# Weights laid out by the host, low parts of the FFN pieces on GpSimd, and a smaller preparing section

## The chip, the cores and the metric

The kernel runs on one core of a Trainium2 chip. The metric is the device time of one execution in microseconds (us). A core has TensorE (PE, matmuls; PEld is its weight load), VectorE (DVE), ScalarE (ACT), GpSimd (POOL) and SyncE (SP), which here only issues DMAs. Each engine takes its instructions in the order in which the program lists them and waits on semaphores.

## The reference

`x` has 4 x 2048 tokens of 512 channels. One layer: token-shifted linear attention with decay per head (32 heads of 16), then an FFN of 2048 hidden channels.

```python
xx = pad(ln(x))[:, :T] - ln(x);  xk, xv, xr, xg = ln(x) + xx * time_maa_{k,v,r,g}
r, k, v = xr @ Wr.T, xk @ Wk.T, xv @ Wv.T;  g = silu(xg @ Wg.T)
# chunks of Q tokens: yc = (rc @ kc * w_mat) @ vc + rc @ state * wb;  state = ws * state + kc * wk @ vc
x = x + (groupnorm(y) * gamma + beta) * g @ Wo.T
D = gelu(fp16(ln(x)) @ W0.T + bias0);  x = x + fp16(fp16(D) @ W1.T + bias1)
```

## The kernel before, in words

The kernel works in fp16 pairs: every weight and most activations are split into a high part (fp16 of the scaled value) and a low part (fp16 of what is left), and each product is made in three passes (two for the FFN).

**The preparing section** (`prepare()`) is a block of its own with a barrier behind it that all engines pass together. It loads x of the first 256 tokens and the five attention weights (1 MB each), has ACT square each for its scale (L493), PE average the sums over partitions (L504), DVE turn this into a power of two (`dve_scale`, six small operations). PE transposes each weight from rows to columns (L617; V is centred by the same matmul, L615), ACT writes the high half from PSUM (L516), and DVE the low half (L423); eight of the ten DVE halves stand in the section, the two of O behind it. SP also issues the loads of the eight 512 KB pieces of W0.

**The steps.** Behind the barrier each engine runs a list of steps n = 0 to 34, written out by hand (`pe_step`, `dve_step`, `act_step`, `pool_step`, `sp_step`). A step handles attention for block n of 256 tokens, the tail of attention of block n-1 and the FFN of block n-2. So steps 0 and 1 have no FFN work yet, and from step 3 on (`*_steady`) all steps are alike. In one step DVE does, among others: `mixf` (L279, 16 of them, from `dx` and `xnT`), low parts of `mix` (L339), `dx` (L270), `att32` (L1350, "weigh", from PSUM), low parts of `att` (L1356), the state S (L1382, four of 64 columns per chunk, four chunks), and y from PSUM (L1400, L1411, L1413). POOL makes the low part of `vw` (L2002), of the gated y (L1982) and of S (`Shl`, L1988). The low part of S after chunk c is waited for by DVE's S of chunk c+1 and by PE's `pe_from_state`.

**The FFN weights** come as 16 pieces (8 of W0, then 8 of W1), prepared in steps 0 and 1 at the places of `PREPARED_AT`: ACT writes the scaled high part (L828) and, for the first nine, a diagonal matrix of the scale (L819). PE makes the transposed low part as piece x diagonal minus high x identity (L847, L851), ACT copies it out of PSUM (L862), and SP transposes the high part by DMA (L872) and stores pieces 5 to 15 to `w_dram` (L882), from where they are streamed each step. DVE and ACT use `xh`, `e16` and `vw32` as places for high parts.

Of the kernel before, what the change touches and what calls it, by code (L numbers as in the profile page):

```python
# [12 lines left out]
P = 128  # L13
# [81 lines left out]
def program(nc, ctx, a, consts, x, out, wd, nb):  # L95
# [33 lines left out]
    maa = sb("maa", [P, 4, G])  # L129
# [7 lines left out]
    gam = sb("gam", [P, G])  # L137
    bet = sb("bet", [P, G])
# [3 lines left out]
    b0 = sb("b0", [P, NH])  # L142
# [14 lines left out]

    B = ps("B", [P, C])
# [206 lines left out]
    def parts_of(q):  # L365

        return place_of(q)[:, 0:2 * C], place_of(q)[:, 2 * C:4 * C]

    def stashed(j):

        return 32 if j < KEPT else 64

    def sp_raw(eng, n, j):
        if n == 0:
            source = W0[2 * P * j:2 * P * (j + 1), :]
        else:
            if j >= KEPT:
                eng.wait_ge(s_stash[j], 32)
            source = W1[:, 2 * P * j:2 * P * (j + 1)]
        if n == 0:  # L380
            eng.dma_start(raw_piece(PIECES * n + j).rearrange("p (b c) -> p b c", b=2),
                          source.rearrange("(b p) c -> p b c", p=P)).then_inc(s_raw[j], 16)
        else:
            for i in range(2):
                eng.dma_start(raw_piece(PIECES * n + j)[:, C * i:C * i + C].rearrange("p (b c) -> p b c", b=G),
                              source[:, P * i:P * i + P].rearrange("(b p) c -> p b c", p=P)).then_inc(s_raw[j], 16)

    def act_piece_square(eng, n, j, squares):
        q = PIECES * n + j
        eng.wait_ge(s_raw[j], 48 if n else 16)  # L390
# [52 lines left out]

    def prepare():
# [3 lines left out]
        raw = sb("raw", [P, 5, G, C], F32, own)  # L448
        centring = sb("centring", [P, P], F32, own)
        junk = sb("junk", [P, G * C], F32, own)  # L450
        sums = sb("sums", [P, 5], F32, own)
        means = sb("means", [P, P], F32, own)
# [11 lines left out]
        tp = (F[:, :, :], own.enter_context(nc.psum_tensor("tp1", [P, 2, C], F32))[:, :, :], Y)  # L464
        landed = [own.enter_context(nc.semaphore(f"landed{u}")) for u in range(5)]
        s_tab, s_means, s_sum, s_all, s_tr, s_hi = (
            own.enter_context(nc.semaphore(f"s_{v}")) for v in ("tab", "means", "sum", "all", "tr", "hi"))
        s_scl = [own.enter_context(nc.semaphore(f"s_scl{u}")) for u in ORDER]
# [3 lines left out]
        def full(u):  # L472
            return 16 * (G + 2) if u in (K_, R_) else 16

        def load(eng, u):

            if u in (K_, R_):
# [352 lines left out]
    def pe_prepare(eng, n, place):  # L830

        q = piece(n, place)
        if q is None:
            return
# [1422 lines left out]
```

## Time and profile before

| | us |
|---|---|
| Median of 3 runs (2046.63 to 2051.36) | 2048.89 |
| The profiled execution's own time | 2050.78 |
| Its span | 2049.0 |
| Preparing section, to the first matmul of step 0 | 43.3 |
| Step 0 and step 1 by DVE's list | 63.9 and 64.8 |
| A step of the steady kind | 60.1 |

The span is what the profile covers; the time of the execution is 1.8 us longer. Row times are from the span's start. In a timeline row, "x8" means that eight instructions of one kind ran one behind the other, and the second number is what they took together; the bracket is the engine's idle time ahead of it and what ended that.

### The profile page before, as it was taken

The numbers are of one execution on the slowest core, as the hardware profiler recorded it, in microseconds if no ns is written. First come the engines' busy times: TensorE is split into PE (matmuls) and PEld (weight loads), VectorE is DVE, ScalarE is ACT, GpSimd is POOL, SyncE is SP. The second block draws the span as 40 slices with busy tenths as digits, with TensorE's granted clock in tenths as the row PEclk, the third lists the DMA queues.
The fourth block names the chain that finished last, engine by engine and source line by source line (L and its number), as shares of the span: only waits on it lengthen the run. The fifth ranks groups of instructions, "written<-read, shape, count | busy, mean of one in ns | idle before, by whom it ended". The sixth has DMA issues, their size and how long they took to land.

```text
span 2049.0 us, 64453 instructions
## 1 busy us (share of the span) xinstructions
PE 1999.8 (98%) x27206; PEld 1424.3 (70%) x27206; DVE 1738.7 (85%) x3687; ACT 1293.0 (63%) x2081; POOL 317.5 (15%) x329
## 2 busy tenths in 40 slices
PE   5889999999999999999999999999999999999999
PEld 4767667777666777766777766667776677777676
DVE  7778889888888888888988888888888898888771
ACT  7775566676555677656667656667765666766452
POOL 1011111111111111111111111111111111111110
PEclk8999999999999999999999999999999999999999
DMA  6776666777666677766667766667777666776656
GB/s 217 161 193 194 177 178 182 199 197 196 177 194 171 189 198 195 185 190 189 173 194 202 199 174 186 181 181 202 192 195 184 191 180 185 199 202 177 181 175 191
DMA packets 403216, 385.42 MB, mean 188 GB/s; under 512 B 256880, under 2 KB 304112, under 8 KB 402928
## 3 DMA queue, kind: packets, MB, share of 16 engines
q1 hardware_dynamic: 401296, 381.12, 68.1%
q8 instruction: 215, 3.52, 0.7%
q14 instruction: 73, 0.60, 0.1%
q10 hardware_dynamic: 1632, 0.18, 0.1%
HBM read 232.32 MB, written 22.54 MB: 124 GB/s over the span
## 4 chain that ended last, share of the span: by engine, by line
PE 81%; SPq 4%; DVE 4%; ACT 4%; DMA 3%; issue 2%; POOL 0%; ACTq 0%; DVEq 0%
PE F L1149 19%; PE F L1086 16%; PE B L892 9%; PE B L1053 8%; PE sc L892 7%; PE YT L924 6%; PE YT L892 3%; DMA y<-ygT 3%; PE YT L976 3%; SPq L2044 2%; PE sc L954 2%; PE YT L995 2%; PE YT L1086 1%; PE F L847 1%; PE YT L1025 1%
## 5 line engine op out<-in xcount | busy, mean ns | idle before, releaser
L1149 PE MATMUL F<-ring,hT 128*128 128x512 f16 x1984 | 467.7, 379 | 0.5 <-issue 0.5
L1149 PEld LDWEIGHTS F<-ring,hT 128*128 128x128 f16 x1984 | 189.1, 98 | 198.4 <-issue 0.8
L1086 PE MATMUL F<-xT,kept 128*128 128x256 f16 x2400 | 276.8, 273 | 2.0 <-issue 1.2
L892 PE MATMUL B<-mix,WT 128*128 128x256 f16 x2304 | 267.5, 273 | 0.0
L1785 ACT ACTIVATE hT<-F,b,f_rho 128x256 f16<-128x256 f32 x480 | 243.4, 560 | 37.8 <-PE F L1086 37.7
L1086 PEld LDWEIGHTS F<-xT,kept 128*128 128x128 f16 x2400 | 234.6, 98 | 42.1 <-issue 2.6
L892 PEld LDWEIGHTS B<-mix,WT 128*128 128x128 f16 x2304 | 222.7, 98 | 33.3 <-DVE gT L1389 0.3
L279 DVE SCALAR_TENSOR_TENSOR mixf<-dx,maa,xnT 128x256 f32<-128x256 f32 x512 | 238.7, 527 | 0.1
L1742 ACT ACTIVATE Shl<-S 128x256 f16<-128x256 f32 x128 | 53.1, 415 | 236.2 <-PE YT L995 125.8
L1988 POOL TENSOR_TENSOR Shl<-S,Shl 128x256 f16<-128x256 f32 x128 | 89.2, 697 | 708.5 <-ACT Shl L1742 702.1
L1736 ACT ACTIVATE att<-att 128x512 f16<-128x512 f32 x256 | 147.5, 624 | 67.7 <-DVE att L1350 67.7
L339 DVE TENSOR_TENSOR mix<-mixf,mix 128x1024 f16<-128x1024 f32 x128 | 184.1, 1438 | 3.2 <-ACT mix L335 2.2
L892 PE MATMUL sc<-mix,WT 128*128 128x256 f16 x1536 | 180.4, 275 | 3.0 <-PEq L577 3.0
L1356 DVE TENSOR_TENSOR att<-att 128x512 f16<-128x512 f32 x256 | 166.8, 693 | 17.2 <-ACT att L1736 17.0
L924 PE MATMUL YT<-WT,mix 128*128 128x512 f16 x768 | 178.6, 383 | 1.3 <-DVE mix L339 0.9
L1086 PE MATMUL F<-xT,ring 128*128 128x256 f16 x1440 | 172.5, 273 | 4.1 <-ACT hT L1785 4.1
L1053 PE MATMUL B<-WT,yg 128*128 128x512 f16 x768 | 176.5, 379 | 0.0
L1350 DVE TENSOR_TENSOR att<-sc,wmask 128x512 f32<-128x512 f32 x256 | 164.3, 684 | 13.3 <-PE sc L954 13.1
L892 PEld LDWEIGHTS sc<-mix,WT 128*128 128x128 f16 x1536 | 151.0, 99 | 34.6 <-issue 3.6
L1993 POOL TENSOR_TENSOR x<-e,x 128x512 f32<-128x512 f16 x62 | 70.7, 1161 | 578.0 <-DVE e L1429 578.0
L1086 PEld LDWEIGHTS F<-xT,ring 128*128 128x128 f16 x1440 | 135.3, 98 | 23.3 <-issue 6.4
L335 ACT ACTIVATE mix<-mixf 128x1024 f16<-128x1024 f32 x128 | 134.6, 1051 | 5.1 <-DVE mixf L279 4.2
(208 smaller groups left out, 3108.6 us busy)
## 6 DMA issues: line engine op xcount, KB each, us to landing
ring<-w_dram SPq DMA_DIRECT2D x352, 512.0 KB, 3.7
kx<-kT SPq DMA_DIRECT2D x96, 256.0 KB, 3.8
rx<-rT SPq DMA_DIRECT2D x96, 256.0 KB, 4.5
xa<-in_L_attn_x SPq DMA_DIRECT2D x32, 512.0 KB, 5.0
vbd<-vN SPq DMA_DIRECT2D x256, 64.0 KB, 2.1
x<-in_L_attn_x SPq DMA_DIRECT2D x32, 512.0 KB, 5.0
out<-x SPq DMA_DIRECT2D x31, 512.0 KB, 3.5
kept<-in_L_ffn_W SPq DMA_DIRECT2D x5, 512.0 KB, 12.0
```

The costliest lines, as they stand in the source:

```text
L279: last = eng.scalar_tensor_tensor(out=mixf[:, m % 2, g, :], in0=dx[:, g, :], scalar=maa[:, m, g:g + 1], in1=xnT[:, g, 1:BT + 1], op0=ALU.m ...
L335: eng.activation(mix[:, m % 2, 0, :, :], mixf[:, m % 2, :, :], ACT.Copy).then_inc(s_mh, 1)
L339: eng.tensor_tensor(mix[:, m % 2, 1, :, :], mixf[:, m % 2, :, :], mix[:, m % 2, 0, :, :], ALU.subtract).then_inc(s_ml, 1)
L892: mm = eng.matmul(out[:, gg * BT:(gg + 1) * BT], WT[:, w, a, kk, rows(g)], mix[:, m % 2, b, kk, :], start=(i == 0 and kk == 0), stop=(i == ...
L924: mm = eng.matmul(Y[:, t, :], mix[:, 0, a, kk, rows(t)], WT[:, V_, b, kk, :], start=(i == 0 and kk == 0), stop=(i == 2 and kk == G - 1))
L1053: mm = eng.matmul(B[:, :], yg[:, a, kk, rows(t)], WT[:, O_, b, kk, :], start=(i == 0 and kk == 0), stop=(i == 2 and kk == G - 1))
L1086: mm = eng.matmul(up_place(f, j)[:, i * BT:(i + 1) * BT], w, xT[:, :, kk, :], start=(kk == 0 and a == 0), stop=(kk == G - 1 and a == 1))
L1149: mm = eng.matmul(F[:, t, :], hT[:, k, rows(t)], ring[:, use % RING, i, a * C:(a + 1) * C], start=(k == 0 and a == 0), stop=(k == NH - 1 a ...
L1350: eng.tensor_tensor(att32[:, x, :], sc[:, x, :], wmask[:, 8 * x:8 * x + 8, :].rearrange("p q i -> p (q i)"), ALU.mult).then_inc(s_am, 1)
L1356: eng.tensor_tensor(att[:, c % 2, 1, C * x:C * x + C], att32[:, x, :], att[:, c % 2, 0, C * x:C * x + C], ALU.subtract).then_inc(s_al, 1)
L1736: eng.activation(att[:, c % 2, 0, C * x:C * x + C], att32[:, x, :], ACT.Copy).then_inc(s_ah, 1)
L1785: eng.activation(hT[:, k, :], up_place(f, j)[:, i * BT:(i + 1) * BT], ACT.Gelu, bias=b0[:, k:k + 1], scale=f_rho[:, j:j + 1]).then_inc(s_h, 1)
```

## The change

- The host lays out all weights but Wv with input channels on partitions, already permuted, and W0 and W1 piece by piece; maa, gamma, beta and bias0 come as one table `cols`. Wr and Wk are one DMA each instead of six.
- In the preparing section PE transposes nothing; it only centres V. High and low halves of K and R are made there from SBUF. Those of V, G and O move into step 0 (`act_late_hi`, `dve_late_lo`). `dve_scale` for V, G and O is one set of six operations on three columns. POOL's memsets of S, Shl, kx, rx and vbd move into the section.
- PE's, ACT's and SP's share in the low parts of FFN pieces goes: no L847, L851, L819, L862, and no DMA transposes. POOL makes each with two instructions (`pool_low`): the piece times its scale, 1024 columns in fp32, in place, then minus the high part, into fp16. Pieces 0 to 4 stand behind `vw` of step 0, 5 and 6 behind `Shl` of chunk 0, 7 behind that of chunk 1; step 1 has 8 to 11, 12 and 13, 14, 15 in the same way.

```diff
+HIGH_AT = ({"X": (2,), "V1": (3,), "sc0": (4,), "state0": (5,), "sc1": (6,), "sc2": (7,)},
+           {"X": (8, 9), "V1": (10,), "sc0": (11,), "G0": (12,), "sc1": (13,), "state1": (14,), "sc2": (15,)})
+LOW_AT = ({"vw1": (0, 1, 2, 3, 4), "state0": (5, 6), "state1": (7,)},
+          {"vw1": (8, 9, 10, 11), "state0": (12, 13), "state1": (14,), "state2": (15,)})
...
+    def pool_low(eng, n, place):
+        if n < 2:
+            for q in LOW_AT[n].get(place, ()):
+                k = min(q, PIECES)
+                eng.wait_ge(s_phi, q + 1)
+                eng.tensor_scalar(raw_piece(q), raw_piece(q), f_scl[:, k:k + 1], None, ALU.mult).then_inc(s_psc, 1)
+                eng.wait_ge(s_psc, q + 1)
+                eng.tensor_tensor(low_place(q), raw_piece(q), high(q), ALU.subtract).then_inc(s_plo, 1)
...
@@ the preparing section, ACT
                 for half in range(2):
                     act_hi(eng, R_, half)
-                act_square(eng, G_)
-                act_hi(eng, V_, 0)
-                act_square(eng, O_)
-                act_hi(eng, V_, 1)
                 act_exps(eng, 1)
                 act_fades(eng)
-                for half in range(2):
-                    act_hi(eng, G_, half)
+                act_square(eng, G_)
                 act_mix_hi(eng, 0, 1)
-                for half in range(2):
-                    act_hi(eng, O_, half)
+                act_square(eng, O_)
@@ the preparing section, DVE
-                dve_scale(eng, V_)
                 for half in range(2):
                     dve_lo(eng, R_, half)
-                dve_lo(eng, V_, 0)
-                dve_scale(eng, G_)
-                dve_lo(eng, V_, 1)
-                dve_scale(eng, O_)
-                for half in range(2):
-                    dve_lo(eng, G_, half)
                 dve_tables_rest(eng)
+                dve_scale(eng, V_)
@@ dve_step, step 0 (places in its order)
                 mix_lo(eng, 0, 1)
+                for half in range(2):
+                    dve_late_lo(eng, V_, half)
...
-                dve_weight_lo(eng, O_, 0, Y)
...
-                dve_weight_lo(eng, O_, 1, F[:, :, :])
...
                 dve_factors(eng)
+                for half in range(2):
+                    dve_late_lo(eng, G_, half)
...
             dve_take_y(eng, n, 1)
+        if n == 0:
+            for half in range(2):
+                dve_late_lo(eng, O_, half)
@@ pool_step
                 eng.tensor_tensor(vw[:, t, 1, :], vw32[:, :], vw[:, t, 0, :], ALU.subtract).then_inc(s_vwl, 1)
+            pool_low(eng, n, "vw1")
...
                 pool_state_lo(eng, n, c)
+                pool_low(eng, n, f"state{c}")
```

POOL's queue before, from the barrier to the first `Shl` of step 1 (`vw` is the weighted V, `Shl` the parts of the state, `yg` the gated y):

```order
L2204 MEMSET vbd 128x2048
L2002 ISA
L2002 TENSOR_TENSOR vw<-vw 128x512 x2
L1988 TENSOR_TENSOR Shl<-S,Shl 128x256 x4
L2002 TENSOR_TENSOR vw<-vw 128x512 x2
L1982 TENSOR_TENSOR yg<-ygT,yg 128x4x128 x2
L1988 TENSOR_TENSOR Shl<-S,Shl 128x256 x4
```

The same queue now, in step 0 (the line of dots stands for the pairs of pieces 1 to 4, which read like that of piece 0):

```order
L1924 TENSOR_TENSOR vw<-vw 128x512 x2
L797 TENSOR_SCALAR ring<-ring,f_scl 128x1024
L799 TENSOR_TENSOR kept<-ring,kept 128x1024
...
L1910 TENSOR_TENSOR Shl<-S,Shl 128x256
L797 TENSOR_SCALAR hT<-hT,f_scl 128x1024
L799 TENSOR_TENSOR hT<-hT,e 128x1024
L797 TENSOR_SCALAR hT<-hT,f_scl 128x1024
L799 TENSOR_TENSOR hT<-hT,xh 128x1024
L1910 TENSOR_TENSOR Shl<-S,Shl 128x256
L797 TENSOR_SCALAR x<-x,f_scl 128x1024
L799 TENSOR_TENSOR x<-x,e 128x1024
L1910 TENSOR_TENSOR Shl<-S,Shl 128x256 x2
```

Ten instructions of 1024 columns now stand between the low part of `vw` and that of the first `Shl`, four between the first and the second `Shl`, two between the second and the third.

PE's list before, in step 0 from the second V product to the second scores (`sc`):

```order
L924 MATMUL YT<-WT,mix 128x512 x12
L847 MATMUL F<-xT,kept 128x128 x4
L851 MATMUL F<-minus_one,e 128x128 x4
L847 MATMUL F<-xT,kept 128x128 x4
L851 MATMUL F<-minus_one,e 128x128 x4
L954 MATMUL sc<-rx,kx 64x64 x32
L847 MATMUL F<-xT,kept 128x128 x4
L851 MATMUL F<-minus_one,vw 128x128 x4
L847 MATMUL F<-xT,kept 128x128 x4
L851 MATMUL F<-minus_one,vw 128x128 x4
L1025 MATMUL YT<-vw,kN 64x64 x48
L892 MATMUL B<-mix,WT 128x256 x24
```

And now, at the same place:

```order
L851 MATMUL YT<-WT,mix 128x512 x12
L881 MATMUL sc<-rx,kx 64x64 x32
L952 MATMUL YT<-vw,kN 64x64 x48
L819 MATMUL B<-mix,WT 128x256 x24
L881 MATMUL sc<-rx,kx 64x64 x32
```

The sixteen matmuls for a piece are gone from each of the eight places of the step, and nothing takes their place on PE.

## Rows read from the trace of the kernel before

**Rows 1.** The page: the span, and each engine's busy time

```profile
span 2049.0 us, 64453 instructions
PE 1999.8 (98%) x27206; PEld 1424.3 (70%) x27206; DVE 1738.7 (85%) x3687; ACT 1293.0 (63%) x2081; POOL 317.5 (15%) x329
```

**Rows 2.** Windows: length, busy PE, PEld, DVE, ACT, POOL, clock, DMA, GB/s

```profile
0.00:43.30 43.30, 20.39 (x114) 19.36 (x115) 29.01 (x85) 30.36 (x48) 0.67 (x7) 0.86 0.82 257
43.30:107.20 63.90, 56.81 (x863) 48.66 (x864) 49.30 (x115) 50.62 (x82) 10.96 (x11) 0.93 0.70 148
107.20:172.00 64.80, 57.36 (x851) 45.65 (x850) 51.54 (x119) 43.63 (x64) 8.13 (x8) 0.95 0.77 189
226.20:286.30 60.10, 60.10 (x835) 42.34 (x834) 53.27 (x112) 38.67 (x62) 9.86 (x10) 1.00 0.70 190
```

**Rows 3.** The chain that ended last, step 0: start, us, what

```profile
82.17 1.03 ACT kept L862
83.34 1.13 PE F L847 x8
```

**Rows 4.** Timeline of the preparing section, ACT, DVE and PE

```profile
8.49 2.02 ACT L527 ACTIVATE wmask<-tabs,ep 128x64 f32<-128x64 f32 x8 [0.44 <-DVE ep L539]
11.83 1.91 ACT L493 ACTIVATE junk<-raw 128x2048 f32<-128x2048 f32 x1 [1.32 <-DMA raw<-in_L_attn_Wk]
20.33 1.28 DVE L423 SCALAR_TENSOR_TENSOR WT<-F,scl,WT 128x1024 f16<-128x1024 f32 x1
42.69 0.06 DVE L575 MEMSET flag<- 128x5 f32 x1
43.32 7.93 PE L892 MATMUL sc<-mix,WT 128*128 128x256 f16 x48 [3.03 <-PEq L577]
51.08 2.78 PE L892 MATMUL B<-mix,WT 128*128 128x256 f16 x24
```

**Rows 5.** Timeline of SP's queue in the preparing section

```profile
30.27 9.55 SPq L596 DMA_DIRECT2D b<-in_L_ffn_bias  x1
```

**Rows 6.** Timeline of DVE, step 0

```profile
67.53 0.69 DVE L1333 TENSOR_TENSOR vw<-YT,wk 128x512 f32<-128x512 f32 x1 [0.76 <-PE YT L924]
69.55 2.12 DVE L270 TENSOR_TENSOR dx<-xnT 128x1024 f32<-128x1024 f32 x1
71.71 3.26 DVE L279 SCALAR_TENSOR_TENSOR mixf<-dx,maa,xnT 128x256 f32<-128x256 f32 x8
74.89 1.28 DVE L1350 TENSOR_TENSOR att<-sc,wmask 128x512 f32<-128x512 f32 x2
```

**Rows 7.** Timeline of DVE, step 1

```profile
107.22 1.66 DVE L279 SCALAR_TENSOR_TENSOR mixf<-dx,maa,xnT 128x256 f32<-128x256 f32 x4
130.16 1.29 DVE L1315 TENSOR_TENSOR ygT<-ygT,gT 128x512 f32<-128x512 f32 x2 [1.58 <-ACT ygT L1705]
170.45 1.29 DVE L1419 BATCH_NORM_STATS2 f_bn<-x 128x6 f32<-128x512 f32 x2
```

**Rows 8.** Timeline of POOL: sizes, alone and beside DVE

```profile
43.68 1.81 POOL L2203 MEMSET kx<- 128x2048 f32 x1
69.44 1.15 POOL L2002 TENSOR_TENSOR vw<-vw 128x512 f16<-128x512 f32 x1 [3.75 <-ACT vw L1697]
84.90 0.67 POOL L1988 TENSOR_TENSOR Shl<-S,Shl 128x256 f16<-128x256 f32 x1 [14.30 <-ACT Shl L1742]
144.32 2.72 POOL L1982 TENSOR_TENSOR yg<-ygT,yg 128x512 f16<-128x512 f32 x2 [14.78 <-ACT yg L1729]
147.00 1.12 POOL L1988 TENSOR_TENSOR Shl<-S,Shl 128x256 f16<-128x256 f32 x1
265.65 2.28 POOL L1982 TENSOR_TENSOR yg<-ygT,yg 128x512 f16<-128x512 f32 x2 [3.60 <-ACT yg L1729]
```

**Rows 9.** Timeline of DVE beside the last three of those

```profile
145.32 2.27 DVE L1356 TENSOR_TENSOR att<-att 128x512 f16<-128x512 f32 x2 [2.28 <-ACT att L1736]
148.22 0.87 DVE L1382 SCALAR_TENSOR_TENSOR S<-S,ws,kv 128x64 f32<-128x64 f32 x4 [0.30 <-POOL Shl L1988]
266.09 2.31 DVE L1382 SCALAR_TENSOR_TENSOR S<-S,ws,kv 128x64 f32<-128x64 f32 x4
```

More of the change, by code:

```diff
@@ L463, in prepare @@
         diag = sb("diag", [P, NT * 8, Q], F32, own)
[L464 to L468, printed above, removed]
+        s_tab, s_sum, s_all = (own.enter_context(nc.semaphore(f"s_{v}")) for v in ("tab", "sum", "all"))
@@ L807, in dve_piece_scale, with stores_of_half @@
             dve_power(eng, i, s_pscl, POW2_PER * k, most, f_rho[:, at], f_scl[:, at])
-    def act_minus_one(eng):
-        eng.activation(minus_one[:, :], ident[:, :], ACT.Copy, scale=-1.0).then_inc(s_minus, 1)
+    def stores_of_half(q):
+        return sum(1 for p in range(KEPT, q) if p % 2 == q % 2)
     def act_high(eng, q):
@@ L1425, in dve_e @@
         eng.wait_ge(s_dn, 8 * (f + 1))
+        if f == 0:
+            eng.wait_ge(s_b, 16)
         for t in range(NT):
@@ L1662, in dve_step @@
             dve_take_y(eng, n, 1)
+        if n == 0:
+            for half in range(2):
+                dve_late_lo(eng, O_, half)
         if tail:
@@ L1856, in act_step @@
             return
-        squares = ygT[:, :, :].rearrange("p g t -> p (g t)").bitcast(F16)[:, 0:2 * C]
         if n == 0:
-            for j in range(4):
-                act_piece_square(eng, 0, j, squares)
+            for half in range(2):
+                act_late_hi(eng, V_, half)
+            for j in range(2):
+                act_piece_square(eng, 0, j)
         if att_n:
@@ L1863, in act_step @@
         if n == 0:
-            act_minus_one(eng)
-            act_piece_square(eng, 0, 4, squares)
+            for j in range(2, 5):
+                act_piece_square(eng, 0, j)
         if n == 1:
@@ L1874, in act_step @@
         if n == 0:
-            act_piece_square(eng, 0, 5, squares)
-            act_piece_square(eng, 0, 6, squares)
+            for half in range(2):
+                act_late_hi(eng, G_, half)
+            act_piece_square(eng, 0, 5)
+            act_piece_square(eng, 0, 6)
         if n == 1:
-            act_piece_square(eng, 1, 5, squares)
+            act_piece_square(eng, 1, 5)
         if ff and not att_n:
@@ L1965, in act_step @@
             if n == 0:
-                act_piece_square(eng, 1, 2, squares)
+                act_piece_square(eng, 1, 2)
             else:
                 act_weights_hi(eng, n, 3)
-            act_prepare(eng, n, "sc3")
             if n == 0:
-                act_piece_square(eng, 1, 3, squares)
+                for half in range(2):
+                    act_late_hi(eng, O_, half)
+                act_piece_square(eng, 1, 3)
             act_state_hi(eng, n, 3)
             if n == 0:
-                act_piece_square(eng, 1, 4, squares)
+                act_piece_square(eng, 1, 4)
             act_square(eng, n, 1)
@@ L2242 @@
     arrays, aps, consts = {}, {}, {}
-    for name in _INS:
-        v = np.ascontiguousarray(inputs[name])
+    for name, v in laid_out(inputs).items():
         arrays[f"in_{name}"] = v
```

436 lines of the change are left out of this document (185 added, 251 removed).

## The prediction, written before the changed kernel had run

> **What bounds the kernel now.** I read the page first, then the windows, the chain, and the timelines. The page has PE busy for 98% of the span [rows 1], and the windows say where the rest is: a steady step is 60.1 us with PE busy for all of it, so nothing there gets shorter by this change, and its instructions are the same before and after [rows 2]. What can move is the time until the steady steps begin: the preparing section of 43.3 us, step 0 of 63.9 and step 1 of 64.8 [rows 2]. In steps 0 and 1 no engine is full (PE 56.8 of 63.9, DVE 49.3, ACT 50.6, POOL 11.0), so chains through several engines set the length. The chain of step 0 runs through the preparation of pieces: ACT's copy out of PSUM, then PE's eight matmuls, and so on [rows 3]. The section before it is closed by DVE's last small operation at 42.69, and PE's first matmul follows at 43.32 [rows 4]. Step 2 and what follows I take as moved by whatever step 1 ends late or early.
>
> **The preparing section.** ACT squares K at 11.83, for which it waits for six DMAs [rows 4]. With one DMA the weight is there earlier, and the square follows the exponentials at 8.49 + 2.02 = 10.5: 1.3 us gained. From there on two lists alternate. DVE now has behind its scale of K (14.3): exponent tables 2.2, table 0.6, dx 1.15, four mixf 1.6, K low 2 x 1.27 (1.28 for one [rows 4]), scale R 1.1, four mixf, low mix 1.15, R low 2.55, tables 2.3; that is 31.1. ACT has the high halves of K at 18, square R, high mix, square V, the high halves of R at 25.4, exponentials to 27.7, square G, high mix, square O to 32.4. The last scale waits for that: 0.7 for PE's mean and 1.1 for six operations, so the section ends at 34.2 where it ended at 42.7: **-8.5**. The other queue that could hold it is SP's: its last DMA is issued for 9.55 us, until the load queue has drained [rows 5]. The window has 257 GB/s over 43.3 us, 11.1 MB, which at some 390 GB/s take 28.5 us; from a start at 3 that ends at 31.7, under 34.2. If it ends later than that, the gain is 5 instead of 8.5.
>
> **Step 0 up to the first weigh.** Before it is 74.89 - 43.32 = 31.6 us [rows 4, 6]. PE's eight preparations are gone, but ACT and DVE are what the first half waits for. DVE has four low halves (V, G) where it had two (O): +2.5. ACT has two high halves of V and two of G more, 4.1, and three diagonals and a copy less, 1.5, and it waits for DVE's scale as before. By the order of the lists I find `vw` of the second tile at 62, its low part on POOL at 63.8 to 64.95, and dx held by it till 66.0, where it ended at 71.67 [rows 6]. So 5.7 of the 8.5 are left here.
>
> Then comes what is new. POOL has four pieces ready (high parts 0 to 3 are made ahead), two instructions each. Its price: the low part of 256 columns takes 0.67 and of 512 columns 1.15 [rows 8], so 1.9 ns for a column and 2.1 us for 1024. For the scaling no row has the form. Below it stands the memset of 2048 columns in 1.81, which gives 0.9 for 1024; above it the two-input instruction with 2.1. I take 1.1, as it reads and writes one column where the memset only writes. A piece is then 3.2 us, 8 of them 26 us in each of the two steps, where POOL was busy for 11.0 and 8.1 [rows 2].
>
> **What this costs DVE.** The rows show POOL and DVE taking turns. At 144.32 POOL's two `yg` take 2.72 instead of 2 x 1.15, and the `Shl` behind them 1.12 instead of 0.67; DVE's two low parts of att, 1.3 when alone, take 2.27 [rows 8, 9]. The four S beside two `yg` take 2.31 instead of 0.87: one of them got in between, and the next waited for the whole second `yg` [rows 8, 9]. dx beside `vw` takes 2.12 [rows 6] where its data take 1.2. All of these DVE instructions read two operands in SBUF. The weigh, which reads PSUM, keeps its length. The Trainium skill has this as a lock: in "SBUF — State Buffer", section "Who interferes with whom", a DVE instruction with two SBUF inputs and a GpSimd instruction that reads SBUF exclude each other for a whole instruction, and the same page sends such work off the critical path. The trace agrees (2.31 against 0.87), and by this rule the change is dearer than by busy time, since POOL's 26 us do not only fill idle time.
>
> So eight mixf (3.26 in a row now [rows 6]) meet eight POOL instructions, and each gives way to one of them: 8 x 0.4 + 8 x 1.5 less a little overlap, 14.4 us: 66.0 to 80.4, where 3.3 would do. The first weigh stands at 80.4 instead of 74.89. The stretch from PE's first matmul (34.8) is 45.6 instead of 31.6: **+14.0**, of which 11.1 is this turn-taking.
>
> **Step 0, the rest.** Piece 4 waits for ACT's high part behind that weigh, and `Shl` of chunk 0 comes behind it on POOL, at 87.6 to 88.2 (84.90 before [rows 8]). PE's scores and ACT's copies no longer wait for preparations, but the S of chunk 1 meets pieces 5 and 6 (S ends at 95.5 instead of 90), piece 7 meets low parts of att, and the end of y is at 113.0. Two low halves of O, 2.55, stand behind it. DVE begins step 1 at 115.6. That is 35.2 for the 32.3 from 74.89 to 107.22 [rows 6, 7]: **+2.9**.
>
> **Step 1.** Up to the gated y it has the same work: 107.22 to 130.16 [rows 7] becomes 115.6 to 138.5. There two gated, dx and eight mixf (5.5 us of DVE) meet pieces 8 to 10 (9.6 us of POOL): the weigh behind them comes at 151.7 instead of 144.1. Pieces 11 to 15 are met by 16 S, 8 low parts of att and 2 of mix, but there DVE had gaps (51.5 busy of 64.8 [rows 2]), which PE's preparations made and which they leave: +1.6. The end of the block's statistics (170.45 + 1.3 and 0.3 [rows 7]) goes from 172.0 to 189.5: **+9.2** for the step.
>
> **The sum.** -8.5 + 14.0 + 2.9 + 9.2 = +17.6 us. On the profiled 2050.8 that is 2068.4. This execution was 1.9 above the median of the three, so the median should be 2066.5. I say **2066**.
>
> Costed at nothing: the DMA loads in larger pieces (covered, the loads lead their readers by several us), the stores of pieces (the first streamed piece is read about 35 us behind the last store; without that cover 3 us), the memsets on POOL (they run beside the wait for x). PE's clock: the 48 matmuls of K behind the barrier take 7.93, and the next 24 take 2.78 [rows 4], so behind a pause the first 24 run at the lower of its two levels, 1.2 GHz, and take 5.2. That stays. PE has more pauses now, so one or two more products may take 5.2 instead of 2.7: 0 to +5, in the range.
>
> **The rivals.**
> - *The turns cost little, and GpSimd's own queue is the limit.* If DVE gets through its short instructions between POOL's, only the order on POOL counts: the end of step 0 is 100, and step 1 ends 17 earlier than now, at 155, since PE and ACT are free of the pieces. The time is 2050.8 - 17 - 1.9 = **2032**. For it speaks that POOL waits for a semaphore between its two instructions, a gap in which DVE may pass more than one mixf. Against it speaks 2.31 for four S [rows 9]. It decides if DVE passes three or more per gap. Chance 0.22. This is the one that ends faster.
> - *The two about cancel*: DVE passes two per turn (half of 11.1 + 7.6 gone, -9) and the gaps in step 1 take up more. Sum near 0 to +5, time 2047 to 2053. Chance 0.15.
> - *The scaling on GpSimd costs like a two-input instruction*, 2.1: 16 us more POOL time, of which some 12 lie in the stretches where DVE waits: **2079**. For it: no row of the form. Chance 0.13. The Trainium skill, "GPSIMD Engine Reference", section "Engine selection", calls one-input work roughly line-rate, which by itself would put the scaling near the lower bound and leave the sum as it is; it also advises DVE for elementwise work.
> - *The section does not shrink*, as SP's last DMA holds the barrier: +3.5, time 2070. It is inside the forecast's range.
>
> **How the numbers follow.** Forecast as above, 2055 to 2076, chance 0.50 with the last rival. About 0.2% (4 us) is what a measurement of this kernel can tell from no change. Faster by more than that: the first rival and a little of the second, 0.27. Same: 0.09. Slower: 0.64. The range that leaves 2 in 10 out reaches from 2034, most of the first rival's case, to 2080. The likeliest case's own range is 2055 to 2076.
>
> **What would show it.** PE's first matmul of step 0 at about 34.8. mixf x8 of step 0 in 12 to 15 us instead of 3.26, with POOL's pairs between. A POOL scaling of 1.1 alone. `Shl` of chunk 0 at 87 to 88. DVE's step 1 from about 115, step 3's first matmul (226.2 now) at 244. The forecast is wrong if mixf x8 takes under 6 us, or if POOL's instructions are themselves much shorter than 2.1.

## The result, and the profile after

The change makes the kernel slower: 2071.27 us (median of 4 runs, 2068.24 to 2076.21) against 2049.63 (4 runs, 2046.63 to 2051.36), ratio 1.0113, 95% interval 1.0098 to 1.0129. That is +21.6 us, or 21.2 between the two profiled executions. The forecast was +17.6, 2066; its direction, its range and nearly its size held. Its inside did not: two terms were wrong by 8 us each, in opposite directions, so that the total came out near is in good part luck. The experiments below say more than the sum.

The page of the changed kernel (its span, each engine's busy time, the granted clock in 40 slices, and the chain by engine), to be read beside [rows 1]:

```profile
span 2070.2 us, 63406 instructions
PE 1969.0 (95%) x26758; PEld 1385.3 (67%) x26758; DVE 1759.0 (85%) x3675; ACT 1276.7 (62%) x2055; POOL 402.5 (19%) x360
PEclk9677999999999999999999999999999999999999
PE 77%; DVE 4%; POOL 4%; SPq 4%; ACT 3%; DMA 3%; issue 2%; ACTq 0%; DVEq 0%
```

PE has 31 us less work and the program takes 21 us more. POOL has 85 us more, all of it in slices 1 to 4. The windows of the same stretches as in [rows 2] (length, busy PE, PEld, DVE, ACT, POOL, clock, DMA, GB/s):

```profile
0.00:37.90 37.90, 10.94 (x50) 10.12 (x50) 22.21 (x69) 24.20 (x42) 6.13 (x10) 0.93 0.77 292
37.90:118.80 80.90, 48.12 (x697) 35.49 (x698) 62.98 (x120) 48.78 (x74) 47.92 (x22) 0.70 0.38 111
118.80:192.40 73.60, 44.45 (x625) 28.30 (x624) 65.74 (x119) 33.90 (x52) 49.98 (x24) 0.72 0.36 112
246.40:306.50 60.10, 59.59 (x831) 41.86 (x830) 52.93 (x111) 38.82 (x62) 9.70 (x10) 1.00 0.67 189
```

The preparing section is 5.4 us shorter, step 0 is 17.0 longer, step 1 is 8.8 longer, and the steady step has its 60.1 us as before. POOL is busy for 48 and 50 us of the two steps where it had 11 and 8, against the 26 + 11 and 26 + 8 forecast. PE has lost its 16 matmuls per place, and its granted clock in those steps has gone from 0.93 and 0.95 to 0.70 and 0.72.

POOL's groups by shape (busy, mean ns of one, idle before):

```profile
L797 POOL TENSOR_SCALAR x<-x,f_scl 128x1024 f32<-128x1024 f32 x2 | 5.7, 2843 | 0.0
L799 POOL TENSOR_TENSOR kept<-ring,kept 128x1024 f16<-128x1024 f32 x5 | 10.9, 2184 | 0.4
```

The subtraction costs what was worked out from [rows 8] (2.1). The scaling costs 2.84, outside the bounds of 0.9 and 2.1 that the prediction drew for it. A piece is 5.1 us of POOL instead of 3.2.

DVE around the first weigh, and where it waits later in step 0 (start, us, what; idle before and what ended it):

```profile
66.50 2.13 DVE L284 TENSOR_TENSOR dx<-xnT 128x1024 f32<-128x1024 f32 x1
68.66 6.72 DVE L293 SCALAR_TENSOR_TENSOR mixf<-dx,cols,xnT 128x256 f32<-128x256 f32 x8
75.31 1.27 DVE L1267 TENSOR_TENSOR y_att<-sc,wmask 128x512 f32<-128x512 f32 x2
76.95 3.54 DVE L1299 SCALAR_TENSOR_TENSOR S<-S,ws,kv 128x64 f32<-128x64 f32 x4
...
95.91 1.65 DVE L1299 SCALAR_TENSOR_TENSOR S<-S,ws,kv 128x64 f32<-128x64 f32 x4 [10.26 <-POOL Shl L1910]
97.48 1.21 DVE L353 TENSOR_TENSOR mix<-mixf,mix 128x1024 f16<-128x1024 f32 x1
...
116.18 2.66 DVE L428 SCALAR_TENSOR_TENSOR WT<-y_gate,scl,WT 128x1024 f16<-128x1024 f32 x2
118.76 0.48 DVE L293 SCALAR_TENSOR_TENSOR mixf<-dx,cols,xnT 128x256 f32<-128x256 f32 x1
```

The eight mixf take 6.72 us where 3.26 stood in [rows 6] and 14.4 was forecast. The four S of chunk 0 take 3.54, where they took 0.87 before. Then the S of chunk 1 wait 10.26 us for `Shl`, which has five pieces ahead of it on POOL:

```profile
67.52 3.82 POOL L797 TENSOR_SCALAR ring<-ring,f_scl 128x1024 f32<-128x1024 f32 x1
71.43 2.42 POOL L799 TENSOR_TENSOR kept<-ring,kept 128x1024 f16<-128x1024 f32 x1
...
90.13 2.85 POOL L797 TENSOR_SCALAR ring<-ring,f_scl 128x1024 f32<-128x1024 f32 x1
93.06 2.12 POOL L799 TENSOR_TENSOR kept<-ring,kept 128x1024 f16<-128x1024 f32 x1
95.14 0.67 POOL L1910 TENSOR_TENSOR Shl<-S,Shl 128x256 f16<-128x256 f32 x1
```

In step 1, DVE meets the pieces again (the four S of chunk 1 took 0.87 before):

```profile
142.90 7.73 DVE L293 SCALAR_TENSOR_TENSOR mixf<-dx,cols,xnT 128x256 f32<-128x256 f32 x8
150.56 1.27 DVE L1267 TENSOR_TENSOR y_att<-sc,wmask 128x512 f32<-128x512 f32 x2
...
163.28 3.13 DVE L1299 SCALAR_TENSOR_TENSOR S<-S,ws,kv 128x64 f32<-128x64 f32 x4
...
190.86 1.29 DVE L1336 BATCH_NORM_STATS2 f_bn<-x 128x6 f32<-128x512 f32 x2
```

How a mixf fares beside each of POOL's two instructions is best seen one by one. Start and end of single instructions of that stretch, from the same trace:

```
POOL scaling      67.52  71.34      (dx holds it until 68.6)
DVE  mixf 1       68.66  69.89      1.22 long
DVE  mixf 2 to 6  69.81  71.87      0.47 each, one behind the other
POOL subtraction  71.43  73.84
DVE  mixf 7       71.79  74.13      2.34 long
POOL scaling      73.83  76.84
DVE  mixf 8       74.05  75.38      1.33 long
```

Beside the subtraction a mixf waits for its end. Beside the scaling it is held for only 0.8 to 0.9 us, and the ones behind it pass freely while the rest of it runs.

### The profile page after: what moved, and what is told of

Its sections match the earlier page's. It is cut to its first block, busy times and chain, and to the rows that moved or that the text cites. A ratio compares the mean times of both kernels' runs of the same rounds, so it can differ in the third digit from the quotient of the medians.

```text
span 2070.2 us, 63406 instructions
## 1 busy us (share of the span) xinstructions
PE 1969.0 (95%) x26758; PEld 1385.3 (67%) x26758; DVE 1759.0 (85%) x3675; ACT 1276.7 (62%) x2055; POOL 402.5 (19%) x360
## 4 chain that ended last, share of the span: by engine, by line
PE 77%; DVE 4%; POOL 4%; SPq 4%; ACT 3%; DMA 3%; issue 2%; ACTq 0%; DVEq 0%
PE F L1078 19%; PE F L1015 16%; PE B L819 9%; PE B L984 8%; PE sc L819 7%; PE YT L851 5%; PE YT L819 3%; DMA y_att<-y_gate 3%; PE YT L903 2%; SPq L1968 2%; PE sc L881 2%; POOL ring L797 1%; PE YT L922 1%; PE YT L1015 1%; PE YT L952 1%
## 5 line engine op out<-in xcount | busy, mean ns | idle before, releaser
L819 PE MATMUL B<-mix,WT 128*128 128x256 f16 x2304 | 274.8, 277 | 7.7 <-DVE gT L1306 7.7
L1706 ACT ACTIVATE hT<-F,cols,f_rho 128x256 f16<-128x256 f32 x480 | 244.1, 562 | 37.7 <-PE F L1015 37.6
L819 PEld LDWEIGHTS B<-mix,WT 128*128 128x128 f16 x2304 | 226.3, 99 | 44.7 <-DVE gT L1306 8.1
L293 DVE SCALAR_TENSOR_TENSOR mixf<-dx,cols,xnT 128x256 f32<-128x256 f32 x512 | 246.7, 542 | 0.1
L1658 ACT ACTIVATE att<-y_att 128x512 f16<-128x512 f32 x256 | 147.7, 625 | 75.3 <-DVE y_att L1267 75.3
L819 PE MATMUL sc<-mix,WT 128*128 128x256 f16 x1536 | 182.9, 277 | 6.0 <-DVE y_att L1267 4.3
L1273 DVE TENSOR_TENSOR att<-y_att,att 128x512 f16<-128x512 f32 x256 | 172.9, 716 | 16.2 <-ACT att L1658 15.8
L984 PE MATMUL B<-WT,y_gate 128*128 128x512 f16 x768 | 181.0, 386 | 5.9 <-DVE x L1239 4.5
L851 PE MATMUL YT<-WT,mix 128*128 128x512 f16 x768 | 179.9, 385 | 3.8 <-DVE mix L353 3.4
L819 PEld LDWEIGHTS sc<-mix,WT 128*128 128x128 f16 x1536 | 152.5, 99 | 38.5 <-issue 6.2
L1267 DVE TENSOR_TENSOR y_att<-sc,wmask 128x512 f32<-128x512 f32 x256 | 164.1, 682 | 11.5 <-PE sc L881 11.3
L1299 DVE SCALAR_TENSOR_TENSOR S<-S,ws,kv 128x64 f32<-128x64 f32 x384 | 134.2, 410 | 13.6 <-POOL Shl L1910 10.3
```

The costliest lines, as they stand in the source:

```text
L293: last = eng.scalar_tensor_tensor(out=mixf[:, m % 2, g, :], in0=dx[:, g, :], scalar=maa[:, m, g:g + 1], in1=xnT[:, g, 1:BT + 1], op0=ALU.m ...
L819: mm = eng.matmul(out[:, gg * BT:(gg + 1) * BT], WT[:, w, a, kk, rows(g)], mix[:, m % 2, b, kk, :], start=(i == 0 and kk == 0), stop=(i == ...
L851: mm = eng.matmul(Y[:, t, :], mix[:, 0, a, kk, rows(t)], WT[:, V_, b, kk, :], start=(i == 0 and kk == 0), stop=(i == 2 and kk == G - 1))
L984: mm = eng.matmul(B[:, :], yg[:, a, kk, rows(t)], WT[:, O_, b, kk, :], start=(i == 0 and kk == 0), stop=(i == 2 and kk == G - 1))
L1267: eng.tensor_tensor(att32[:, x, :], sc[:, x, :], wmask[:, 8 * x:8 * x + 8, :].rearrange("p q i -> p (q i)"), ALU.mult).then_inc(s_am, 1)
L1273: eng.tensor_tensor(att[:, c % 2, 1, C * x:C * x + C], att32[:, x, :], att[:, c % 2, 0, C * x:C * x + C], ALU.subtract).then_inc(s_al, 1)
```

## The experiments

Theories. **A**: GpSimd's queue is too long, so that `Shl`, and what ScalarE does behind the low parts, come late. **B**: turns, a DVE instruction with two inputs in SBUF and a GpSimd instruction hold each other. **C**: TensorE's lower clock costs it. All kernels are the changed one with the edit shown. "Before" is the kernel before, timed on the same chip.

### e1: no low parts at all

```diff
-                eng.tensor_scalar(raw_piece(q), raw_piece(q), f_scl[:, k:k + 1], None, ALU.mult).then_inc(s_psc, 1)
-                eng.wait_ge(s_psc, q + 1)
-                eng.tensor_tensor(low_place(q), raw_piece(q), high(q), ALU.subtract).then_inc(s_plo, 1)
+                eng.memset(low_place(q).bitcast(F32), 0.0).then_inc(s_plo, 1)
```

> Left out: the low parts of all 16 FFN pieces; in the place of GpSimd's two instructions per piece stands one memset of the low place (512 words, some 0.5 us). Everything else is the changed kernel. Both theories (A: GpSimd's queue of 5.1 us per piece makes the low part of S late; B: turn-taking holds DVE's two-input instructions) say that what the pieces cost goes: mixf x8 of step 0 back from 6.7 to 3.3, no wait of S of chunk 1 for Shl (10.3 us), end of step 0 at about 101 instead of 118.8, step 3 some 28 us earlier: 2071 - 28 = 2043, range 2035 to 2050. A third theory (C: the loss is PE's clock, granted 0.7 in both steps) says that little comes back: 2060 or more.

Measured: 2038.12 (before 2049.4), ratio 0.9943 [0.9926, 0.9961]. So GpSimd's pieces cost 33 us of time for 81 us of its work. Without any low parts the kernel is 11.5 us faster than before; that isn't what the rest of the change is worth, since the kernel before makes the low parts too (e10 compares like with like). Little is left for C: the granted clock goes up to 0.77 in step 0 and 0.86 in step 1, still far below that of before, but the nine long products of the two steps that ran at the lower clock in the changed kernel, wholly or in part (4.1 to 5.1 us each, 42.0 together), still take 39.0 here, and 33 us came back.

### e2: subtraction alone, and e3: scaling alone

e2 leaves out the `tensor_scalar` and its wait; e3 puts e1's memset in the place of the subtraction.

> Left out: the scaling of the pieces; the subtraction stays (so the low parts are of unscaled pieces). A piece costs GpSimd 2.2 us instead of 5.1. A (queue): pieces 0 to 4 end at 79, before the S of chunk 0, so the wait of S of chunk 1 goes nearly whole, and the time is within 6 us of the kernel without lows (2043 to 2050). B (turns): the subtraction is what holds DVE for all of its length, so most of the cost stays: 2060 to 2066.

> Left out: the subtraction; the scaling in place stays, with a memset of the low place (512 words) behind it. A piece costs GpSimd 2.85 + 0.5 = 3.4 us. A (queue): pieces 0 to 4 end at 84.5, 4 us behind the first S, and step 1's pieces are 27 us long: 5 to 10 us above the kernel without lows, 2048 to 2054, dearer than the subtraction alone. B (turns): the scaling holds a DVE instruction for only 0.8 us, so it is cheaper than the subtraction alone: 2043 to 2048.

Measured: e2 2055.19, ratio 1.0034 [1.0021, 1.0046]; e3 2049.95, ratio 1.0005 [0.9993, 1.0016]. Over e1 the subtraction costs 17.1 us and the scaling 11.8, though the scaling is the longer instruction. Neither theory forecast both: e2 lies between the ranges of A (2043 to 2050) and B (2060 to 2066), and e3 has the time that A gave it and the order, cheaper than the subtraction, that B gave it. Their sum, 28.9, leaves 4.3 of the 33.2 for the two together. DVE and POOL in e2:

```profile
68.49 10.59 DVE L293 SCALAR_TENSOR_TENSOR mixf<-dx,cols,xnT 128x256 f32<-128x256 f32 x8
79.01 1.27 DVE L1265 TENSOR_TENSOR y_att<-sc,wmask 128x512 f32<-128x512 f32 x2
67.33 9.89 POOL L797 TENSOR_TENSOR kept<-ring,kept 128x1024 f16<-128x1024 f32 x4
```

and DVE in e3:

```profile
68.68 3.99 DVE L293 SCALAR_TENSOR_TENSOR mixf<-dx,cols,xnT 128x256 f32<-128x256 f32 x8
72.60 1.27 DVE L1267 TENSOR_TENSOR y_att<-sc,wmask 128x512 f32<-128x512 f32 x2
87.17 1.65 DVE L1299 SCALAR_TENSOR_TENSOR S<-S,ws,kv 128x64 f32<-128x64 f32 x4 [7.34 <-POOL Shl L1910]
```

These are the two mechanisms, nearly apart. In e2 four mixf alternate with four subtractions, 2.34 us each (one and only one mixf gets in between), then four run at 0.4: 10.59. In e3 the mixf lose 0.7 us in all, and it is mostly the queue that costs. The times at which DVE reaches the same marks, read from its timelines:

| | first weigh | S of chunk 1 ends | end of y | first f_bn of step 1 ends |
|---|---|---|---|---|
| e1, none | 71.98 | 80.13 | 98.97 | 161.10 |
| e2, subtraction | 79.01 | 90.93 | 108.10 | 176.33 |
| e3, scaling | 72.60 | 88.83 | 105.83 | 171.51 |
| changed kernel | 75.31 | 97.56 | 116.26 | 191.55 |

### e4: ScalarE scales, and e12: the subtraction in smaller instructions

```diff
@@ act_high (e4, e12)
+        eng.wait_ge(s_phi, q + 1)
+        eng.activation(raw_piece(q), raw_piece(q), ACT.Identity, scale=f_scl[:, k:k + 1]).then_inc(s_psc, 1)
@@ pool_low (e4, e12)
-                eng.tensor_scalar(raw_piece(q), raw_piece(q), f_scl[:, k:k + 1], None, ALU.mult).then_inc(s_psc, 1)
@@ pool_low (e12 alone)
+                parts = 4 if q < KEPT else 1
+                for i in range(parts):
+                    at = slice(2 * C // parts * i, 2 * C // parts * (i + 1))
+                    last = eng.tensor_tensor(low_place(q)[:, at], raw_piece(q)[:, at], high(q)[:, at], ALU.subtract)
...
```

> Whole computation. The scaling in place is moved from GpSimd to ScalarE, which does it behind the high part of the piece (1.1 us each, 16 times); GpSimd has the subtraction alone, 2.2 us per piece. A (queue): ScalarE waits 8 us twice in step 0, so most of the 17.6 us there are covered; 2048 to 2056. B (turns): 2062 to 2070.

> e4 (scaling by ScalarE, subtraction by GpSimd), whole computation, where the subtraction of pieces 0 to 4 is four instructions of 256 columns instead of one of 1024. If DVE and GpSimd give way to each other for one whole instruction each time (B), a mixf then waits for 0.6 instead of 1.9 us: the eight mixf beside them take 8 x 0.4 + 8 x 0.6 = 8.0 us instead of the 10.6 of e2 and e4, and GpSimd, which gives way to each of them too, takes 16 x 0.67 + 3 = 14 us for what took it 9.9. The time is then 2 us under e4's 2064 to 2 above, since the S behind them has 4 us of GpSimd's queue more. If a turn has a length of its own, or DVE is held until GpSimd's row of instructions ends, the eight mixf take 10.6 or more.

Measured: e4 2064.06, ratio 1.0068 [1.0051, 1.0086]; e12 2062.94, ratio 1.0065 [1.0051, 1.0078]. Taking 45 us of work from GpSimd gave 7 us back, as B said (2062 to 2070). e4's first weigh is even later than the kernel's, 81.86, as the subtractions now stand back to back and its mixf take 10.59 again. In e12 the same eight mixf stand beside subtractions of 256 columns:

```profile
71.06 6.44 DVE L293 SCALAR_TENSOR_TENSOR mixf<-dx,cols,xnT 128x256 f32<-128x256 f32 x8
...
69.89 15.94 POOL L803 TENSOR_TENSOR kept<-ring,kept 128x256 f16<-128x256 f32 x20
```

10.59 becomes 6.44 (8.0 expected), with every mixf but the first 0.88 us long and one POOL instruction to each: a turn here is as long as the instruction on the other side. The time hardly followed. The first weigh came 4.4 us earlier, and step 1, where the pieces have no parts, ended 2.8 earlier; 1.1 remain at the end, within the spread of the runs.

### e5: another order on GpSimd

```diff
-LOW_AT = ({"vw1": (0, 1, 2, 3, 4), "state0": (5, 6), "state1": (7,)},
+LOW_AT = ({"vw1": (0, 1), "state0": (2, 3), "state1": (4, 5), "state2": (6,), "state3": (7,)},
```

> Whole computation, the same instructions; only GpSimd's order in step 0 differs: pieces 0 and 1 behind vw, 2 and 3 behind the first Shl, 4 and 5 behind the second, 6 and 7 behind the third and fourth (the kernel: 5, 2, 1). A (queue): the first Shl starts at about 81 instead of 95.1, of the 10.3 us wait little is left, the second one waits for 2 pieces as before; step 0 ends 6 to 10 us earlier, 2062 to 2066. B (turns): as many GpSimd instructions meet as many of DVE, only others; 2069 to 2074.

Measured: 2073.53, ratio 1.0119 [1.0103, 1.0135], no gain over the kernel. `Shl` of chunk 0 starts at 79.22 instead of 95.14 and the S behind it ends at 87.0 instead of 97.6, as A says. Then the time goes again, to another wait of the same queue:

```profile
101.69 1.15 ACT L783 ACTIVATE e<-x,f_scl 128x1024 f16<-128x1024 f32 x1 [8.96 <-POOL hT L799]
...
106.18 1.29 DVE L1273 TENSOR_TENSOR att<-y_att,att 128x512 f16<-128x512 f32 x2 [8.27 <-ACT att L1658]
```

The high part of piece 7 may only be written when low part 5 is made, ScalarE stands there for 8.96 us, and att behind it. The end of y is at 113.7 (116.3 before the edit), and the weigh of step 1 at 150.45 (150.56). This order only moves the wait: eight pieces of 5.1 us still pass in one step, and what no longer waits for them first waits for them later. Other orders, with ScalarE's list changed to match, were not tried.

### e6: TensorE kept busy

Added are matmuls whose product is not read, at the old places of the pieces.

```diff
+    def pe_prepare(eng, n, place):
+        if n < 2:
+            eng.wait_ge(s_wlo, 6)
+            for i in range(2):
+                for b in range(2 * G):
+                    eng.matmul(F[:, i, rows(b % G)], WT[:, K_, 0, b % G, 0:P], WT[:, K_, 0, b % G, P:2 * P],
+                               start=True, stop=True)
...
```

> Whole computation; added are 16 matmuls of 128 columns whose product nobody reads, at each of the eight places of step 0 and seven of step 1 where the kernel before made the low parts of pieces. They keep TensorE busier in the places where it now waits. C (clock): the granted clock of both steps goes from 0.7 to 0.9, the V, G and K products of 4.1 to 5.1 us take 2.8, and 4 to 8 us come back: 2063 to 2067. A and B: the products at the lower clock lie beside the waits for GpSimd and DVE; within 2 us of the kernel, 2069 to 2073.

Measured: 2072.38, ratio 1.0119 [1.0101, 1.0137]. The windows of the two steps:

```profile
37.90:118.00 80.10, 54.33 (x826) 43.03 (x825) 62.90 (x120) 48.62 (x74) 47.82 (x22) 0.79 0.39 113
118.00:191.00 73.00, 49.10 (x733) 33.85 (x731) 65.14 (x115) 33.51 (x52) 49.99 (x24) 0.81 0.37 111
```

The clock rises from 0.70 and 0.72 to 0.79 and 0.81 (not to the 0.9 expected), the steps are 0.6 to 0.8 us shorter, and the time is not. This is only half a test of C. Most long products stayed slow: the nine that took 42.0 us took 38.2, where nine at the full clock would take 25 (2.8 each). What the full clock would give is not shown here. That the clock is not the loss is shown by e1, which got 33 us back with 3.0 us less in those products, and by e11 below, which has 0.78 and 0.81, the clock of e6, and is 21 us faster than the changed kernel.

### e7: the new layout, with low parts by TensorE as before

The core of the edit; places, copies and high parts follow the kernel before.

```diff
+            for b in range(G):
+                at = C * i + P * b
+                eng.matmul(F[:, i, rows(b)], diagonals[:, k % 2, :], raw_piece(q)[:, at:at + P],
+                           start=(b == 0), stop=False)
+            for b in range(G):
+                at = C * i + P * b
+                mm = eng.matmul(F[:, i, rows(b)], minus_one[:, :], high(q)[:, at:at + P],
+                                start=False, stop=(b == G - 1))
...
+        eng.activation(low_place(q), F[:, :, :].rearrange("p k c -> p (k c)"), ACT.Copy).then_inc(s_plo, 1)
```

> Whole computation. The host's layout and the smaller preparing section stay; the low parts of the pieces are made as in the kernel before, by TensorE (diagonal of the scale times piece, minus identity times high part) and a copy by ScalarE, GpSimd has none. No DMA transposes are needed, as the layout is the host's. A and B: GpSimd's pieces cost 33 us over the kernel without lows (2038.1); by TensorE and ScalarE they cost what the two steps of the kernel before had over those without lows, 124.0 - 119.4 = 4.6 us: 2043, range 2040 to 2048, faster than both kernels. C: the same, with the clock back at 0.9, perhaps 2 us less.

Measured: 2055.83, ratio 1.0038 [1.0024, 1.0052]: 15 us better than the changed kernel, but slower than before and 13 above what was expected. The trace shows a wait that none of the theories had (two rows of e7, then the same place in e1):

```profile
128.43 1.04 ACT L830 ACTIVATE ring<-F 128x1024 f16<-128x1024 f32 x1
137.80 1.15 ACT L791 ACTIVATE xh<-ring,f_scl 128x1024 f16<-128x1024 f32 x1 [8.33 <-DMA w_dram<-xh]
...
131.63 1.15 ACT L783 ACTIVATE xh<-ring,f_scl 128x1024 f16<-128x1024 f32 x1 [8.29 <-DMA w_dram<-xh]
```

In all versions of the changed kernel high parts have two places instead of three, and the store that frees the first stands on SP's queue behind eight DMAs of `vbd` and two of 512 KB. As e1 has this wait too, its 2038 is not the least that the layout allows.

### e8 and e9: the small tables of the preparing section

e8 is e7 with a wait for the tables ahead of the identity and R on SP. e9 is the changed kernel with a semaphore of its own for `un`:

```diff
-                eng.dma_start(un[:, :], bonus.rearrange("h o -> (h o)").partition_broadcast(P)).then_inc(s_tab, 16)
+                eng.dma_start(un[:, :], bonus.rearrange("h o -> (h o)").partition_broadcast(P)).then_inc(s_un, 16)
...
-                eng.wait_ge(s_tab, 48)
+                eng.wait_ge(s_tab, 32)
                 eng.activation(en[:, :], en[:, :], ACT.Exp).then_inc(s_e0, 1)
```

> e7 with one wait more: SyncE issues the identity, R and what follows only when ScalarE's three small tables are in. In the changed kernel the first exponential waits until 10.78 for the last of these (7.8 before), behind 1 MB of K and of R. Expected: exponentials at about 8, preparing section 2 to 3 us shorter, PE's first matmul at about 35.3 and 2 to 3 us under e7. Rival: K's loading is what the small ones queue behind, then nothing changes; or R comes too late and it is 1 to 3 us longer.

> The changed kernel, whole computation, with one edit: the last of ScalarE's three small tables (un, needed only by DVE's tables) has a semaphore of its own, so that the exponentials wait for the first two alone. tabs is issued at 1.2 and lands 7.4 later. Expected: exponentials at about 9 instead of 10.8, PE's first matmul at 36.1 instead of 37.9, 1.8 us less in all (2069.5). Rival: ScalarE's list then waits for K, and nothing changes.

Measured: e8 2058.63, ratio 1.005 [1.0035, 1.0065]; that is 2.8 above e7, within their intervals. Its rival held: the first matmul is at 37.78 (e7 37.99) and the first exponential at 10.62 (10.83), though R and the identity are issued only then. So what delays the tables is issued ahead of R; K as one DMA is what differs there from the kernel before, but no run changes K by itself. e9 2069.82, ratio 1.0099 [1.0086, 1.0113]. The first exponential in the changed kernel and in e9:

```profile
10.78 0.23 ACT L635 ACTIVATE en<-en 128x32 f32<-128x32 f32 x1 [5.72 <-DMA un<-in_L_attn_time_faaaa]
```

```profile
8.62 0.23 ACT L636 ACTIVATE en<-en 128x32 f32<-128x32 f32 x1 [3.58 <-DMA tabs<-const_tabs]
```

PE's first matmul in e9 is at 35.8 instead of 37.94, and all marks up to the statistics of step 1 are 2.0 us earlier. Of this the medians show 1.5, which their spread does not tell from nothing.

### e10 and e11: both waits removed, low parts by TensorE or by DVE

Both have e9's edit and this one, which issues two stores earlier; e11 makes each low part with one DVE instruction, spread over its list.

```diff
+        if n == 1:
+            sp_store(eng, PIECES, 0)
+            sp_store(eng, PIECES + 1, 0)
         if att_n:
             sp_vbd(eng, n, 1)
...
@@ e11, dve_piece_lo
+                eng.scalar_tensor_tensor(out=low_place(q), in0=raw_piece(q), scalar=f_scl[:, k:k + 1], in1=high(q),
+                                         op0=ALU.mult, op1=ALU.subtract).then_inc(s_plo, 1)
```

> e7 (low parts by TensorE and ScalarE) with two edits: the edit of e9, and in step 1 SyncE issues the stores of the high parts of pieces 8 and 9 before the DMAs of the second vbd instead of behind them and the loads of x. In e7 ScalarE waits 8.3 us (129.5 to 137.8) for that store before it may write the high part of piece 10 into the same place. If this wait is what e7 has more than the 2043 expected of it: 2 us for the first edit and 5 to 8 for the second, 2047, range 2043 to 2050, and no wait of ScalarE at 130. If it is cover for something else, 2052 to 2055.

> As e10, but the low part of each piece is one instruction of DVE (piece times scale, minus high part: the form that takes 1.28 for a weight half), spread over its list in steps 0 and 1; GpSimd and TensorE have none. 16 x 1.24 = 20 us more DVE work, where GpSimd's way had 80 us of GpSimd. B (turns): what DVE does itself costs only its length, less DVE's idle time (some 8 us in the two steps without lows): 2038.1 - 2 + 12 = 2048, range 2042 to 2056, 23 us under the changed kernel. If 16 such instructions cost as much as GpSimd's, 2066 or more, then it is the added links in the chain and not the turns.

Measured: e10 2048.78, ratio 0.9996 [0.9986, 1.0006]; e11 2050.59, ratio 1.0001 [0.9992, 1.001]. The wait of e7 is gone from e10, and the two edits together are worth 7.0 us:

```profile
126.92 1.04 ACT L831 ACTIVATE ring<-F 128x1024 f16<-128x1024 f32 x1
128.08 1.15 ACT L792 ACTIVATE xh<-ring,f_scl 128x1024 f16<-128x1024 f32 x1
```

And one row of e11's DVE, by shape:

```profile
L795 DVE SCALAR_TENSOR_TENSOR x<-x,f_scl,e 128x1024 f16<-128x1024 f32 x2 | 2.6, 1278 | 0.0
```

What takes GpSimd 5.1 us in two instructions takes DVE 1.28 in one. Sixteen of them leave the time 21 us under the changed kernel, though DVE is the busiest engine of these steps. Neither version beats the kernel before; both match it.

This is also what the rest of the change is worth with the low parts made as before: nothing clear of the spread, though PE's first matmul in e10 is at 35.80 instead of 43.32. The stretch from there to the first weigh (at 71.93) is 36.1 us where it was 31.6: the halves of V and G, which left the preparing section, stand in this stretch now.

## Why the prediction came out right, and where it was wrong

**The sum.** The forecast's own stretches against the trace:

| | forecast | measured | before |
|---|---|---|---|
| preparing section | 34.8 | 37.9 | 43.3 |
| first matmul to first weigh | 45.6 | 37.4 | 31.6 |
| first weigh to step 1 | 35.2 | 43.4 | 32.3 |
| step 1 to the end of the statistics | 73.9 | 73.6 | 64.8 |

The last total is right, the middle two miss by 8.2 each and cancel, and the first makes up 3.1 of the 3.6 between the forecast +17.6 and the profiled +21.2. So the direction was forecast for one true reason (turns) and without the other (the wait for `Shl`), and the size is luck. None of the times named as signs came out: the first matmul at 37.94 (34.8), mixf in 6.72 (12 to 15), the scaling 2.84 (1.1), `Shl` at 95.14 (87 to 88), step 1 from 118.76 (115), step 3 from 246.2 (244).

**Preparing section, -8.5.** It is -5.4. The step that failed is "the square follows the exponentials at 8.49 + 2.02 = 10.5": they start at 11.45, since `un` lands later, with K beside it as one large DMA. The lists behind it were counted right: 26.0 us from the exponentials to DVE's last scale at 37.5, 25.7 forecast. e9 gives 2.1 of the 3.1 back. The forecast had set the exponentials as unmoved though it moved the DMAs next to them. SP's last DMA did not hold the barrier: it is issued in 0.44 us at 23.4, so that rival falls. (The forecast's sum for that queue has a slip: 3 + 28.5 is 31.5, not 31.7.)

**Turn-taking, 14.4 us for eight mixf.** Wrong as put: "each gives way to one of them" holds beside the subtraction alone. They took 6.72, which is 7.7 of the 8.2 that this stretch was forecast too long. With nothing but subtractions (e2) one mixf goes per subtraction, 2.34 for the pair, and the eight end at 10.59 only because the high part of piece 4 is not there and POOL's row breaks off after four. DVE is held beside both instructions, but beside the scaling for 0.8 to 0.9 us of 2.84. The Trainium skill, "SBUF — State Buffer", section "Who interferes with whom", has the lock for a whole instruction; e2 and e12 agree (a turn of 2.3 beside 1024 columns, 0.81 beside 256), the scaling does not. Why it does not, no run shows.

**The scaling, 1.1 us, range 0.9 to 2.1.** It is 2.84, and the upper bound was no bound: an instruction with one input and a scalar read from SBUF was taken to be no dearer than one with two inputs. The rival that it costs 2.1 had the right direction and expected its price in turns; most of it came as queue. It is 2.8 ns a column, against DVE's 1.25 for multiply and subtract together (e11). The Trainium skill, "GPSIMD Engine Reference", section "Engine selection", calls one-input work roughly line-rate, which would have put it near the lower bound; the trace does not agree.

**The queue.** The first rival named it, and joined it to a gain: it is the other half of the loss. `Shl` of chunk 0 came at 95.14 (forecast 87.6) and S of chunk 1 waited 10.26 us for it, a wait that was not in the forecast. e3 shows the queue nearly alone, 11.8 us, e2 turns for the most part, 17.1. e2 has some queue too (`Shl` at 84.68 with S ready at 81.5), so that is not a clean split.

**Step 1, +9.2**: +8.8, and here too two errors cancel. Up to the weigh it took 31.8 us, 36.1 forecast, with 7.73 for eight mixf; that the weigh stood at 150.56 (151.7) is due to the later start. From the weigh to the end of the statistics it took 41.8 instead of 37.8: the gaps did not cover the turns, three groups of four S take 2.7 to 3.1 us where they took 0.87. One thing was missed there: ScalarE waits 7.79 us for the store of a high part (to 147.88). Here it lies beside DVE's turns and seems to cost little, as POOL works through without a pause until 161; no run removes it from this kernel. In e7 it is bare, and its removal, with e9's edit, is 7.0.

**PE's clock, 0 to +5.** Not one or two products run wholly or partly at the lower clock but nine, of 4.1 to 5.1 us, the first V product with 5.12 among them. They lie beside waits for the most part, as e1 shows, where they are nearly as slow.

**The price of e7.** It was forecast from the pieces of the kernel before, which seemed to cost 4.6 us: 128.6 us from the first matmul to the end of step 1's statistics, against 124.0 in e1 (the expectation writes 124.0 and 119.4; the difference is the same). Split at the first weigh, the traces say more:

| | first matmul to first weigh | first weigh to the end of the statistics |
|---|---|---|
| before | 31.6 | 97.1 |
| e1 | 34.0 | 89.9 |
| e10 | 36.1 | 96.8 |

Behind the weigh the pieces by TensorE cost about 7 us in the kernel before and in e10 alike. Ahead of it the kernel before was 2.4 us shorter than e1, with the halves of V and G in its preparing section, and this hid a part of the 7; no run moves these halves back. So 4.6 was a poor price, and the traces of e10 and e1 give 9. The medians put e10 12.7 above 2036, which is an estimate for e1 with e9's edit (2038.1 less 2). The other 3 to 4 may be spread: e10's profile is of its fastest execution (2045.08, median 2048.78).

What stays open: how the 4.3 us arise by which both instructions cost more than the sum of each.

## What to carry to other kernels

Before work is moved to GpSimd because it stands idle, look for two things: whether it shares a stretch with DVE instructions that read two operands in SBUF, and whether it stands ahead of something short that others wait for. Here 81 us of it cost 33, where the same work as 23 us of a busy DVE cost some 15 (e11 against the estimate of 2036). Measure the price of an instruction that the trace doesn't have before building on it, and draw no upper bound from an instruction that merely looks more complex. When a forecast is a sum of two losses, ask which of them each number feeds: with the scaling between the subtractions the first weigh came at 75.31 instead of 79.01 (fewer turns), and S of chunk 1 ended at 97.56 instead of 90.93 (more queue). The total alone would have taught the wrong reason. And work that leaves a preparing section is gained only if the place where it goes has room for it.

## What the runs showed of the hardware

- GpSimd's `tensor_scalar` with the scalar in SBUF, fp32, 1024 columns: 2.84 us. `tensor_tensor` fp32 minus fp16, 1024 columns: 2.12; 256 columns: 0.67. A memset of 512 words: 0.53.
- Beside a row of GpSimd `tensor_tensor`, GpSimd and DVE instructions with two inputs in SBUF alternate strictly, one each: pairs of 2.3 us (1024 columns) and 0.81 us (256 columns) with a mixf of 0.4. Beside the `tensor_scalar` DVE is held for 0.8 to 0.9 us, then runs freely.
- A broadcast DMA of 16 KB issued at 1.65 landed at 10.7 with K's 1 MB issued as one DMA ahead of it; issued at 1.68 with K in six DMAs, and the identity ahead of them, at 7.8. Holding R and the identity back changed nothing (e8).
- Nine products of TensorE that take 2.8 us each at the full clock took 42.0 us together in the changed kernel (granted clock 0.70 and 0.72) and 39.0 in e1 (0.77 and 0.86), which is 33 us faster.
